# Two of a tile's five 128x512 transposes moved off TensorE: y and the mixed rows through DRAM and 32x32 block transposes on VectorE

## What is computed

```
y   = (shared_out + routed_out)                      # MoE output, per token row
h   = gelu(y_in @ w1[sel] + b1[sel])                 # 512 -> 1024, weights of the batch's expert
z   = h @ w2[sel] + b2[sel]                          # 1024 -> 512
x1  = base + 0.3 * (z @ Wo + bo)                     # base = x + y
dx  = x1_previous_token - x1
xk  = x1 + dx * maa_k                                # goes to the hashed experts
xr  = x1 + dx * maa_r
r   = xr @ w_recept.T                                # receptance, used by a later stage
```

## Time and profile before

| | |
|---|---|
| runs, median of 3 | 2510.55 us (2509.78 to 2514.25) |
| profiled execution, first to last instruction (span) | 2502.9 us |
| TensorE busy | 2451.8 us (98%) |
| VectorE, ScalarE, GpSimd busy | 1148.3, 897.2, 551.4 us |
| DMA | 412.81 MB, mean 165 GB/s |

### The profile page before, as it was taken

How to read it: one execution, slowest core, us unless ns; L and a number is a source line. 1 busy time by engine, 2 the same in 40 slices (tenths; PEclk the granted TensorE clock), 3 DMA queues, 4 the chain that set the end, 5 groups by cost and what they waited for, 6 DMA issues and landing times. The chain is left out here.

```text
span 2502.9 us, 40913 instructions
## 1 busy us (share of the span) xinstructions
PE 2451.8 (98%) x12556; PEld 2046.1 (82%) x12557; DVE 1148.3 (46%) x1771; ACT 897.2 (36%) x1459; POOL 551.4 (22%) x498
## 2 busy tenths in 40 slices
PE   8999999999999899999999989999999999999999
PEld 4778888888899688888888878998978888888877
DVE  5655555325343344344434356766643333332356
ACT  2233333216555222222222246666642222222234
POOL 1100000002222276666657510000011111111100
PEclk9999999999999999999999999999999999999999
DMA  8698898317466433363343266665641011110025
GB/s 297 210 329 310 301 318 317 141 44 269 150 238 223 172 120 111 114 255 108 113 171 127 92 235 230 239 227 222 241 141 43 25 34 30 29 34 25 25 101 185
DMA packets 135988, 412.81 MB, mean 165 GB/s; under 512 B 29843, under 2 KB 34419, under 8 KB 119394
## 3 DMA queue, kind: packets, MB, share of 16 engines
q1 hardware_dynamic: 108626, 314.20, 35.3%
q0 software_dynamic: 19072, 61.66, 7.7%
q10 hardware_dynamic: 8208, 35.88, 3.7%
HBM read 558.71 MB, written 144.80 MB: 281 GB/s over the span
## 5 line engine op out<-in xcount | busy, mean ns | idle before, releaser
L99 PE MATMUL s_g<-wx_hi,s_x_hi 128*128 128x512 f32 x512 | 203.4, 397 | 2.3 <-DVE s_x_lo L2306 1.6
L101 PE MATMUL s_g<-wx_hi,s_x_lo 128*128 128x512 f32 x512 | 200.2, 391 | 0.0
L100 PE MATMUL s_g<-wx_lo,s_x_hi 128*128 128x512 f32 x512 | 199.5, 390 | 0.0
L2019 DVE TENSOR_TENSOR s_w_lo<-s_w_raw,s_w_hi 128x1024 fp32r<-128x1024 f32 x124 | 146.4, 1222 | 75.3 <-ACT s_w_hi L1948 73.7
L99 PE MATMUL s_g<-s_u,s_c_hi 128*128 128x512 f32 x384 | 152.8, 398 | 1.6 <-PEq L1833 1.6
L101 PE MATMUL s_g<-s_u,s_c_lo 128*128 128x512 f32 x384 | 149.9, 390 | 0.0
L100 PE MATMUL s_g<-s_u,s_c_hi 128*128 128x512 f32 x384 | 149.5, 389 | 0.0
L99 PE MATMUL s_h_ps<-s_x_hi,s_w_hi 128*128 128x256 f32 x512 | 144.9, 283 | 1.7 <-DVE s_x_lo L2044 1.7
L101 PE MATMUL s_h_ps<-s_x_hi,s_w_lo 128*128 128x256 f32 x512 | 144.9, 283 | 0.0
L100 PE MATMUL s_h_ps<-s_x_lo,s_w_hi 128*128 128x256 f32 x512 | 144.9, 283 | 0.0
L2205 POOL DMA_INDIRECT s_y<-mid_hash_out,first_rec x32 | 31.6, 986 | 475.4 <-DMA mid_hash_out<-s_o 392.8
(11 more groups left out here) (411 smaller groups left out, 6814.0 us busy)
## 6 DMA issues: line engine op xcount, KB each, us to landing
s_half<-mid_w ACTq DMA_DIRECT2D x124, 2048.0 KB
s_w_raw<-in_w SPq DMA_DIRECT2D x64, 512.0 KB, 6.2
mid_w<-s_x_grp SPq DMA_DIRECT2D x32, 1024.0 KB, 5.8
mid_w<-s_pool_b SPq DMA_DIRECT2D x32, 1024.0 KB, 4.9
s_half<-mid_w SPq DMA_DIRECT2D x32, 1024.0 KB
s_w_raw<-in_w2h SPq DMA_DIRECT2D x16, 2048.0 KB, 7.4
s_w_raw<-in_w1h SPq DMA_DIRECT2D x15, 2048.0 KB, 7.4
mid_routed<-s_o_sb SPq DMA_DIRECT2D x72, 256.0 KB
```

The costliest lines, as they stand in the source:

```text
L99: pe.matmul(out, a_hi, w_hi, start=first, stop=False, skip_group_check=True)
L100: pe.matmul(out, a_hi, w_lo, start=False, stop=False, skip_group_check=True)
L101: return pe.matmul(out, a_lo, w_hi, start=False, stop=last, skip_group_check=True)
L2019: dve.tensor_tensor(lo[:, c], raw[:, c], hi[:, c], ALU.subtract).then_inc(S[name + "_lo"], 1)
```

## The change

y and xr are no longer turned by TensorE, except y of the first tile and xr of the last two. Instead:

- The engine that makes y or xr writes the 512 features of a row reordered: 4 groups of 128 elements, group g holding the 32-element piece g of each of the four quarters. For y this takes four VectorE instructions instead of one; GpSimd reads or writes xr and y through the reordering views.
- SyncE stores the tile to DRAM and, when the store has landed, loads it back with four DMAs (`load_by_quarters`). DMA g fills 32 partitions with column group g of all 128 rows, in pieces of 512 bytes. y comes back into the buffer z, xr into k_part.
- VectorE turns the 32x32 blocks of the whole tile in one instruction (`turn_quarters`), y into ty_ps (PSUM), xr into a new SBUF tile xrt. ScalarE and VectorE split from there as before.
- SyncE's order becomes rec, store_xr (lag 4), b2, load_xr (lag 4), b1, store_y (lag 1), store_x1, load_y (lag 1), shared, x, store_r.
- New waits: z_add waits for the turn of y (z is shared), GpSimd's k_part for the turn of xr, y's next write for its store.

```diff
+def load_by_quarters(eng, dst, rows, sem):
+    for g in range(P // 32):
+        eng.dma_start(dst[32 * g:32 * g + 32].rearrange("t (s c) -> t s c", c=P),
+                      rows[:, g * P:(g + 1) * P].rearrange("(s t) c -> t s c", t=32)).then_inc(sem, 16)
+def in_order(row):
+    return row.rearrange("p (k g a) -> p k g a", k=DC, g=4)
+def by_quarter(row):
+    return row.rearrange("p (g k a) -> p k g a", g=4, k=DC)
+def turn_quarters(dve, dst, src):
+    return dve.transpose(dst.rearrange("p k (s t) -> p k s t", t=32), src.rearrange("p (s k a) -> p k s a", s=4, a=32))
...
+            def store_y(i, n, turn):
+                if isinstance(i, int) and i == 0:
+                    return
+                wait_apart(sp, S["y"], i + 1)
+                sp.dma_start(y_rows[n], y[:]).then_inc(S["y_sent"], 16)
+            def load_y(i, n, turn):
+                if isinstance(i, int) and i == 0:
+                    return
+                wait_apart(sp, S["tz"], i - 1)
+                wait_apart(sp, S["y_sent"], i * 16)
+                load_by_quarters(sp, z[:], y_rows[n], S["y_quarters"])
+            def store_xr(i, n, turn):
+                if isinstance(i, int) and i >= NB - 2:
+                    return
+                wait_apart(sp, S["xr"], i + 1)
+                sp.dma_start(xr_rows[n], xr[:]).then_inc(S["xr_sent"], 16)
+            def load_xr(i, n, turn):
+                if isinstance(i, int) and i >= NB - 2:
+                    return
+                wait_apart(sp, S["xk"], i + 1)
+                wait_apart(sp, S["xr_sent"], i * 16 + 16)
+                load_by_quarters(sp, k_part[:], xr_rows[n], S["xr_quarters"])
...
-            software_pipeline(sp, NB, [(0, load_rec), (2, load_b2), (1, load_b1), (3, store_x1),
-                                       (0, load_shared), (0, load_x), (5, store_r)], 2)
+            software_pipeline(sp, NB, [(0, load_rec), (4, store_xr), (2, load_b2), (4, load_xr), (1, load_b1), (1, store_y),
+                                       (3, store_x1), (1, load_y), (0, load_shared), (0, load_x), (5, store_r)], 2)
...
+                    wait_for(pool, S["xrt"], min(i, NB - 2) if isinstance(i, int) else i)
                     pool.tensor_tensor(k_part[:], dx[:], maa_r[:], ALU.mult).then_inc(S["r_part"], 1)
...
-                dve.scalar_tensor_tensor(y[:], routed[1][:], rec_f[:, n, GATE2:GATE2 + 1], y_part[:],
-                                         ALU.mult, ALU.add).then_inc(S["y"], 1)
+                for k in range(DC):
+                    last_part = dve.scalar_tensor_tensor(
+                        by_quarter(y[:])[:, k], in_order(routed[1][:])[:, k], rec_f[:, n, GATE2:GATE2 + 1],
+                        in_order(y_part[:])[:, k], ALU.mult, ALU.add)
+                last_part.then_inc(S["y"], 1)
...
+            def turn_y(i, n, turn):
+                if isinstance(i, int) and i == 0:
+                    return
+                dve.wait_ge(S["y_quarters"], i * 64)
+                dve.wait_ge(S["y_lo"], i)
+                turn_quarters(dve, ty_ps[:], z[:]).then_inc(S["ty"], 1)
+            def turn_xr(i, n, turn):
+                if isinstance(i, int) and i >= NB - 2:
+                    return
+                dve.wait_ge(S["xr_quarters"], i * 64 + 64)
+                wait_for(dve, S["xr_lo"], i)
+                turn_quarters(dve, xrt[:], k_part[:]).then_inc(S["xrt"], 1)
...
-                (1, h_lo(0)), (2, x1_), (1, h_lo(1)), (3, hashed_lo(0, 2)),
+                (1, h_lo(0)), (3, turn_xr), (2, x1_), (1, h_lo(1)), (0, turn_y), (3, hashed_lo(0, 2)),
...
-                (3, turn_xr(False)), (0, turn_y), (1, down)], 2)
+                (3, turn_xr(NB - 1)), (0, turn_y), (1, down)], 2)
```

More of the change, by code:

```diff
@@ L1306, in stage_ffn @@
                  "w1_in0 w1_in1 w2_in00 w2_in01 w2_in10 w2_in11 "
-                 "part_y y base x_plus_y ty y_hi y_lo half_y half_ty half_y_hi half_y_lo h_ps h_add gelu th h_hi "
-                 "h_lo mm2 z_add tz z_hi z_lo mmo x1 x1_out prev_in dx k_part xk r_part xr ~xk_sent txr xr_hi "
+                 "part_y y y_sent y_quarters base x_plus_y ty y_hi y_lo half_y half_ty half_y_hi half_y_lo h_ps h_add gelu th h_hi "
+                 "h_lo mm2 z_add tz z_hi z_lo mmo x1 x1_out prev_in dx k_part xk r_part xr xr_sent xr_quarters xrt ~xk_sent txr xr_hi "
                  "xr_lo mmr r_ready ~r_out hashed_in hashed_hi shift shifted ~first_hash0 ~first_hash1")
@@ L1364, in stage_ffn @@
         r_bank = lambda i: last_r_ps[i] if isinstance(i, int) and i in last_r_ps else r_ps
+        y_rows = nc.dram_tensor("mid_y_rows", [2, P, D], FP32, kind="Internal").ap()
+        xr_rows = nc.dram_tensor("mid_xr_rows", [2, P, D], FP32, kind="Internal").ap()
         is_next_to_last = lambda i: isinstance(i, int) and i == NB - 2
@@ L1646, in combine @@
                 dve.wait_ge(S["routed2_in"], i * 16 + 16)
-                wait_for(dve, S["ty"], i)
+                if isinstance(i, int) and i < 2:
+                    wait_for(dve, S["ty"], i)
+                else:
+                    dve.wait_ge(S["y_sent"], i * 16 - 16)
                 wait_for(dve, S["x_plus_y"], i)
@@ L1748, in turn_h, with turn_z @@
                 return stage
[L1750 to L1757, removed]
+            def turn_z(i, n, turn):
+                pe.wait_ge(S["z_add"], i + 1)
+                wait_for(pe, S["z_lo"], i)
+                for k in range(DC):
+                    mm = pe.transpose(tz_ps[:, k], z[:, k * P:(k + 1) * P], ident[:])
+                mm.then_inc(S["tz"], 1)
             def turn_y(i, n, pair):
@@ L1805, in receptance_at, with turn_xr @@
                 return stage
-            def turn_xr(sooner):
+            def turn_xr(which):
                 def stage(i, n, turn_no):
-                    if sooner == (isinstance(i, int) and i == NB - 2):
-                        turn(xr, "xr", tz_ps, "z_lo", -2, "txr")(i, n, turn_no)
+                    if isinstance(i, int) and i == which:
+                        pe.wait_ge(S["xr"], i + 1)
+                        pe.wait_ge(S["z_lo"], NB)
+                        for k in range(DC):
+                            mm = pe.transpose(tz_ps[:, k], xr[:, k * P:(k + 1) * P], ident[:])
+                        mm.then_inc(S["txr"], 1)
                 return stage
@@ L1822, in _ @@
             software_pipeline(pe, NB, [
-                (1, find_weights), (1, up(0)), (2, turn(z, "z_add", tz_ps, "xr_lo", 1, "tz")), (1, up(1)), (1, turn_h(0)),
-                (4, receptance_at(True)), (2, times_wo), (1, turn_h(1)), (3, turn_xr(True)), (2, shift_last),
+                (1, find_weights), (1, up(0)), (2, turn_z), (1, up(1)), (1, turn_h(0)),
+                (4, receptance_at(True)), (2, times_wo), (1, turn_h(1)), (3, turn_xr(NB - 2)), (2, shift_last),
                 (4, receptance_at(False)),
-                (3, turn_xr(False)), (0, turn_y), (1, down)], 2)
+                (3, turn_xr(NB - 1)), (0, turn_y), (1, down)], 2)
 def stage_hashed(nc, ins, d, keep):
```

34 lines of the change are left out of this document (23 added, 11 removed).

## The result

The kernel with the change takes 2605.68 us (median of 4 runs, 2600.18 to 2611.11), the kernel before 2511.51 in the same session: 94 us more, ratio 1.038, 95% interval 1.036 to 1.040. The forecast was 2565.5, 55 more than before, in a range of 2503 to 2615: the direction is right, the size 40 us short, and the time lies beside rival 3's 2608. The profiled execution spans 2599.8 us against 2502.9, so the 97 us are in its trace.

A forecast was written before the change was run, and what follows sets the result against it. TensorE bounds the kernel; after the change y's cycle through x1 and SyncE does. Ordinary periods 19, early steps 7.5, weights 18, start 6.5 and clock 4 total 55: 2510.5 + 55 = 2565.5 us, range 2503 to 2615.

The forecast's parts named there:

- rival 3: SyncE becomes the bound: quarter issues at 0.63 to 0.77 us, period 20.7 to 21.3, about 2608 us; chance 0.25.
- TensorE's own bound: TensorE's instruction stream sets the 18.8 us step; removing both transpose groups saves 0.88 per step, at most 26.8 us.
- The cycle through x1 and SyncE's queue: Loop of up-projection, x1, SyncE, y_lo, next up-projection: period 19.5 us against 18.8, TensorE waiting 1.6 per step.
- Its pieces: Parts of y's loop: four issues of 0.38 us, landing 2.3, block turn 0.69, then y_hi 0.60 and y_lo 0.68.
- The store of y, 2.1: y's store to DRAM lands 2.1 us after its issue, like mid_x of the same shape, early enough for the load.
- xr_lo, as long, fits beside y_hi: On VectorE xr_lo, as long as y_lo (0.68 us), waits behind the turn and runs beside ScalarE's y_hi.
- the forecast's 19: 27 ordinary periods, each 19.5 us instead of 18.8, add 19 us.
- The two early steps 7.5: Two periods from 865.55 to 896.65, without receptance product, go from 31.1 us together to 2 x 19.5: +7.5.
- the start 6.5: y of tile 1 is stored into full DMA traffic, so the up-projection starts at 871.2 instead of 864.6: 6.5 us.
- Expert weights 18: y's quarter loads meet expert weights: 8 us in each of two steps, 2 more in the step after the first.
- Clock 4 in all: TensorE's lower clock after three stalls of 6 to 8 us: 0 to 2.5 each, taken as 4 us in all.
- The ordinary 1.6 us waits: 0: TensorE's 1.6 us waits for y in ordinary steps cost nothing in lower clock.

The follow-up runs named there:

- e_nolanding: Changed kernel, but y's quarter loads fetch the rows stored a step earlier, so none waits for this step's store to land: 2605.5 us, 1.0386 of the kernel before.
- e_yonly: Changed kernel with only the y part; xr is turned by TensorE again, as before: 2583.4 us, 1.0288 of the kernel before.
- e_ylofirst: Changed kernel with y_lo ahead of xr_lo in VectorE's order, nothing else: 2585.56 us, 1.0305 of the kernel before.
- e_noweights: Changed kernel without loads of further experts' weights, every tile using the first expert's: 2574.09 us, 1.0252 of the kernel before.

## Why the prediction was right, and where its size was off

- **TensorE's own bound, 0.88 us per step for both groups: right.** 18.27 with one group gone, 17.88 with both, 0.90 less than 18.78.
- **The cycle through x1 and SyncE's queue: right, to a tenth.** In the step shown, from the up-projection's start: x1 ends at +10.19 (forecast 10.07), hrec's issue ends at +13.54 (13.59), the first quarter goes out at +13.77 (13.79), the turn ends at +17.84 (17.97), TensorE starts at +19.58 (19.5).
- **Its pieces.** Four issues 1.76 (1.52); a quarter lands in 2.0 (2.3); the turn 0.73 (0.69); the four parts of y 1.17 (1.4). The errors cancel. By the figure of the Trainium skill (VectorE: DVE Perf Modes, "The three transpose paths") the turn would have been 1.24, an estimate; the trace doesn't bear that out for a whole fp32 tile in one instruction, into PSUM (0.73) or SBUF (0.70).
- **The store of y, 2.1: wrong, 3.6.** It did no harm in this order, as e_nolanding shows, but it hid that there is a second chain of equal length, and with it how hard the change is to mend.
- **"xr_lo, as long, fits beside y_hi": the term that failed in the ordinary steps.** In 14 of its 30 times it took 1.2 to 1.8 instead of 0.67 and was over after y_hi. What I passed over is an operand: its source was the PSUM tile tz_ps, and the change makes it xrt in SBUF. e_yonly, where the source is tz_ps again, has it at 0.67 beside the same work of GpSimd. Ordinary steps cost 1.7 each, not 0.7 (43 us in 25 steps; the forecast's 19 was for 27). Of the 43, 12 are longer waits behind xr_lo. e_ylofirst takes that term out, 18 to 20 us with the clock that comes with it.
- **The two early steps 7.5, the start 6.5: 11.9 and 9.0.** The same places, dearer: the waits there were 9.0, 4.4 and 3.9, and the clock averaged 0.87 and 0.92 in the two early steps.
- **Expert weights 18: 30.** The place was right, and the cause for 23 of the 30 (e_noweights). I had put 8 for each of two steps and 2 for the one after the first. Against 19.6 they are 10.7 and 11.6, and 7.7 for the one between: its y is stored at 1145.73 into the traffic and its quarters go out only at 1157.33, a stall of its own.
- **Clock 4 in all: some 16.** By the busy time of the steps, eight at the lower clock cost 12 and the early ones some 4; the 0.3 per wait at clock 1.00, 8 us in all, was no term of the sum and is inside the cycle's 19.58. These us are inside the numbers above, not on top of them. "The ordinary 1.6 us waits: 0" was right for waits of 1.3 to 1.5, not for all those of 2.3 to 2.4.
- **xr's part.** I had it off the path but for VectorE's 0.69, and alone it is a gain of 3.5 (interval 2 to 7). That it could hold back h through VectorE in a late step was not among the cases.
- **Rival 3** came within 3 us of the time for another reason: its issues of 0.63 to 0.77 are 0.44, and the longer steps came from VectorE, the weights and the clock. So there is luck in the range: all five terms of the sum (19, 7.5, 18, 6.5 and 4) were too small, and its upper end of 2615 held the time because rival 3, for its own reason, had put it there.

## What to carry to other kernels

A trip through DRAM between two operations of one step has to be laid against the whole step and against every in-order queue that it enters: here it saved TensorE 0.44 us and put some 11 us of latency (store issued at 1193.53, y_lo done at 1204.34) into a loop with 3.7 us of slack. The part whose user comes a step later (xr) gained, the part whose user waits (y) lost. When one wait is removed and nothing moves, look for a second chain of the same length before giving the theory up, and order each engine's work so that what can be late stands last.

## What the runs showed of the chip that I had not expected

- A VectorE subtraction with both inputs in SBUF (xr_lo) took between 0.67 and 1.77 us; the one with an input in PSUM (y_lo) took 0.68 to 0.69 in all 31 steps, and xr_lo with its PSUM source in e_yonly 0.67 to 0.69. The Trainium skill (SBUF — State Buffer, "Who interferes with whom") says just this: a VectorE instruction with two SBUF inputs contends with a GpSimd one that reads SBUF, and one with at most one SBUF input, outside the two-port modes, doesn't. The trace agrees; no run here stopped GpSimd alone to test it by itself.
- Which of the two pays depends on which starts first. In 17 of the 30 steps GpSimd's instruction ran first: it kept its own 1.26 to 1.31 and the subtraction ended 0.55 after it. In the other 13 the subtraction started first or within 0.04 us of it: it took 0.67, and GpSimd's took 1.56 to 1.84 and ended 1.12 later. So 0.1 us of timing decides between 0.67 and 1.7, and the steps come in two kinds.
- The store of y, 256 KB, took 3.6 us to land (median), where mid_x, the same shape, took 2.1, before and in the changed kernel. Why is open.
- The granted clock stayed at 1.00 through eight steps with waits of 1.3 to 1.5 us each, and was at 0.66 in the 5 us after one of 2.4, though not after each of those. It was at 0.92 over the whole of that step, and the step's matmuls took 1.5 us longer.
